# A list scheduler that charges each kind of TensorE tiling change its own delay, in a fused attention and sparse-FFN kernel

## The chip, the cores and the metric

One NeuronCore of a Trainium2 chip runs the whole program. The metric is the device time of one execution in microseconds (us). Before the change it is 773.45 us, the median of three runs (772.93 to 773.46).

## The reference, cut to what matters

```python
xn  = layernorm(x)                                     # x: 2048 x 256, float32
# attention: 8 heads of 32, 2 key/value heads, rotary positions, causal
out = softmax(mask(q @ k.T / sqrt(32))) @ v            # per head
qp, kp = q[..., :3] @ dirs, k[..., :3] @ dirs          # one number a position and head
geo_out = softmax(mask(outer(qp, kp))) @ v             # the "geo" attention
out = (out + head_scales * (geo_out - out)) @ Wo
# feed-forward with ternary weights, 1024 wide
z = xn @ ternary(W_syn).T + b_syn
hidden = where(z >= 102nd largest of its row, relu(z), 0)
ffn = layernorm(xn + hidden @ ternary(W_out).T + b_out)
return x + attention + ffn
```

## The kernel before

**Tiles and stages.** The 2048 positions are 16 tiles of 128, or 4 chunks (`c`) of 512. Per tile, TensorE transposes the normalised input (`xT`), multiplies by the q, k, v weights (`qkv`), and transposes q and k (`qT`, `kT`). To subtract a row maximum in the softmax it first forms all scores once in pieces of up to 512 columns (`S`, line 1110), whose maxima VectorE takes (`red`, lines 929 and 932). The feed-forward has the units `xsT`, `z`, `found`, `hT` and `fo`, and ScalarE and VectorE search each row's threshold between them (`sign`, `pick`, `hide`).

**The attention loop.** A slot is (chunk `c`, key head `g`, `kind`, key tile `j`); there are 160 slots. `kind` 1 is the geo attention, `kind` 0 the ordinary one, and each chunk has both, geo first. In a slot TensorE makes the scores of 4 heads in two `pair`s (two matmuls each: line 1191 for kind 0, line 1195 for geo), ScalarE takes the exponent of each pair (`exp`, line 731), TensorE then does `val` (probabilities times v, line 1209) and `sum` (probabilities times ones, line 1216). `probs` has two buffers, so the exponents of slot n+2 wait for the `sum` of slot n (its semaphore `probs_used`). On the diagonal GpSimd clears a triangle (`cut`, line 608).

**Tilings of TensorE.** The planner knows three modes. "full" is every unit and the ordinary scores. "columns" is `val` and `sum`, whose stationary tile is 32 columns wide, four heads side by side. "rows" is the geo scores, whose contraction is 10 rows; their four heads sit in the row groups 0, 32, 64 and 96.

**What sets the order.** `build_plan()` (line 48) is a list scheduler that runs on the host while the program is built. Its result is the fixed order of the instructions of all five engines, and which PSUM bank each unit uses. Nothing is reordered on the chip: the semaphores only make engines wait. Operations stand in flows (queues of one engine that keep their order); each has a duration, a rank (low goes first) and what it waits for. In each step the head of each flow gets an earliest start, `start = max(ready, clock[eng])`; the earliest over all engines, `first`, chooses the engine; and of the heads of that engine that start within `SLACK` = 120 ns of it the one of lowest rank is placed. Ranks on TensorE: units of attention 0 to 7, `h` units 10, `z` units 11, scores 12, `sum` 12.5, `val` 13. Units have two PSUM banks of their own (`BANKS`); `S` may also use the score banks where the next score waits for something. A hand-over between engines counts `HAND` = 160 ns, one within an engine 40 ns.

A change of mode adds `TURN` to the duration of the operation that was chosen, after the choice is made.

Of the kernel before, what the change touches and what calls it, by code (L numbers as in the profile page):

```python
# [15 lines left out]
HG = H // G  # L16
# [19 lines left out]
BANKS = 2  # L36
PAIRS = 2
HAND = 160
TURN = 110
SLACK = 120  # L40
KINDS = ((1, 0), (1, 0), (1, 0), (1, 0))
ATT_SCALE = float(D) ** -0.5
# [5 lines left out]
def build_plan():  # L48
# [10 lines left out]
    for c in range(NCH):  # L59
        tiles = list(range(TPC * c, TPC * c + TPC))  # L60
        for t in tiles:
            add("stat", "dve", 3, ("stat", t), 650, [("x", c)])
        add("stat", "dve", 3, ("eps", c), 180, [("stat", t) for t in tiles])
        add("prep", "pool", 0, ("rstd", c), 1050, [("eps", c)])
        add("stat", "dve", 3, ("shift", c), 180, [("rstd", c)])
        for t in tiles:
            add("norm", "act", 2, ("xn", t), 400, [("shift", c)])
        for t in tiles:
            old = [("unit", "qT", t - 1, 1), ("unit", "kT", t - 1)] if t else []
            unit("qkv", 2 * c, ("xT", t), 220, [("xn", t)])  # L70
            add("xnT", "act", 1, ("xnT", t), 400, [("unit", "xT", t)] + [("unit", "qkv", t - 1)] * (t > 0), empties=("xT", t))
            unit("qkv", 2 * c, ("qkv", t), 1300, [("xnT", t)] + [("w",)] * (t == 0) + [("unit", "kT", t - 2)] * (t > 1))
            add("rope", "dve", 0, ("rope", t), 1380, [("unit", "qkv", t)] + [("join", t - 1)] * (t > 0),
                empties=("qkv", t))
            add("rope", "dve", 0, ("split", t), 1050, [("join", t), ("q_twin", t)] + old[1:])
            add("twin", "act", 1, ("q_twin", t), 620, [("join", t)] + old[:1])
            add("prep", "pool", 1, ("join", t), 880, [("rope", t)] + [("split", t - 1), ("q_twin", t - 1)] * (t > 0))
            add("prep", "pool", 1, ("geo_dots", t), 1300, [("join", t)] + old[1:])
            for half in range(2):
                unit("heads", 2 * c, ("qT", t, half), 440, [("split", t), ("q_twin", t)])  # L80
            unit("heads", 2 * c, ("kT", t), 440, [("split", t), ("geo_dots", t)])
            wait = [("sum", c - 2, G - 1, 0, TPC * (c - 1) - 1)] if c >= 2 else []
            for half in range(2):
                add("heads", "act", 1, ("q_in", t, half), 590, [("unit", "qT", t, half)] + wait, empties=("qT", t, half))
            add("heads", "act", 1, ("k_in", t), 800, [("unit", "kT", t)] + [("geo_hi", c - 1), ("geo_max", c - 1), ("geo_lo", c - 1)] * (c > 0),
                empties=("kT", t))
        for t in tiles:
            for h in range(H):
                for p in range(c + 1):
                    cols = CHUNK if p < c else (t % TPC + 1) * P  # L90
                    unit("S", 2 * c + 1, ("S", t, h, p), 25 + 0.41 * cols, [("q_in", t, h // HG), ("k_in", t)])
                    add("S", "dve", 1, ("red", t, h, p), 152 + 1.045 * cols + (20 if p == c else 0), [("unit", "S", t, h, p)],
                        empties=("S", t, h, p))
            add("S", "dve", 1, ("mx", t), 180, [("unit", "mT", c - 1)] * (c > 0 and t == tiles[0]))
        unit("S", 0, ("mT", c), 440, [("mx", t) for t in tiles])
        add("S", "dve", 1, ("m", c), 1400, [("unit", "mT", c)] + [("m_dma", c - 1)] * (c > 0), empties=("mT", c))
        add("dma", "sp", 0, ("m_dma", c), 1000, [("m", c)])

        add("geo", "dve", 3, ("scan", c), 2800, [("k_in", t) for t in tiles] + [("geo_top", c - 1)] * (c > 0))
        add("geo", "act", 2, ("geo_hi", c), 1050, [("k_in", t) for t in tiles] + [("geo_dma", c - 1)] * (c > 0))  # L100
        add("geo", "dve", 3, ("geo_lo", c), 1220, [("geo_hi", c)])
        add("geo", "pool", 3, ("geo_max", c), 2650, [("scan", c)])
        add("geo", "dve", 3, ("geo_top", c), 1830, [("geo_max", c)] + [("geo_dma", c - 1)] * (c > 0))
        add("geo", "sp", 1, ("geo_dma", c), 8000, [("geo_top", c), ("geo_lo", c), ("geo_hi", c), ("fill",)]
            + ([("sum", c - 1, G - 1, 1, TPC * c - 1)] if c >= 1 else []))
# [41 lines left out]
    for n, (c, g, kind, j) in enumerate(slots):  # L147
        share = 1 - max(0, j - TPC * c) / TPC
        for pair in range(PAIRS):
            first = [("m_dma", c)] if kind == 0 else [("geo_dma", c)]  # L150
            old = [("exp",) + slots[n - 1] + (pair,)] if n else []
            add("score", "pe", 12, ("score", c, g, kind, j, pair), (475 if kind == 0 else 225) * share + 15, first + old,
                "full" if kind == 0 else "rows")
            add("exp", "act", 0, ("exp", c, g, kind, j, pair), 170 + 855 * share, [("score", c, g, kind, j, pair)]
                + ([("sum",) + slots[n - 2]] if n >= 2 else []))
            if j >= TPC * c:
                add("cut", "pool", 0, ("cut", c, g, kind, j, pair), 440, [("exp", c, g, kind, j, pair)])
        e = epilogues.index((c, g, kind))
        add("val", "pe", 13, ("val", c, g, kind, j), 30 + 870 * share,
            [("cut" if j >= TPC * c else "exp", c, g, kind, j, PAIRS - 1)]  # L160
            + ([("o_raw",) + epilogues[e - 1], ("d_raw",) + epilogues[e - 1]] if j == 0 and e else []), "columns")
        add("val", "pe", 12.5, ("sum", c, g, kind, j), 30 + 870 * share, [("val", c, g, kind, j)], "columns")
    for e, (c, g, kind) in enumerate(epilogues):
        last = [("sum", c, g, kind, TPC * (c + 1) - 1)] + [("mix",) + epilogues[e - 1]] * (e > 0)
        add("epi", "act", 0, ("d_raw", c, g, kind), 600, last)
# [40 lines left out]
    mode = "full"  # L206
# [4 lines left out]
    while left:  # L211
        best = []
        for (eng, flow), keys in queue.items():
            at = heads[(eng, flow)]
            if at == len(keys):
                continue
            key = keys[at]
            rank = ranks[key]
            _, ns, after, m, empties = op[key]
            ready = 0.0  # L220
            ok = True
            if key[0] in ("o_add", "y_out"):
                other = ("y_out" if key[0] == "o_add" else "o_add", key[1])
                if other in done:
                    after = after + (other,)
            if any(d not in done for d in gates.get(key, ())):
                continue
            for d in after:
                if d not in done:
                    ok = False  # L230
                    break
                src = op[d][0] if d in op else "sp"
                ready = max(ready, done[d] + (40 if src == eng else HAND))
            if not ok:
                continue
            if key[0] == "unit":
                spare = [i for i in banks_for(key) if free_from(i) is not None]
                if not spare:
                    continue
                ready = max(ready, min(free_from(i) for i in spare))  # L240
            if key[0] == "score":
                pair = [free_from(BANKS + 2 * key[5] + i) for i in range(2)]
                if None in pair:
                    continue
                ready = max(ready, max(pair))
            start = max(ready, clock[eng])
            best.append((start, rank, key, eng, flow, ns, m))
        first = min(b[0] for b in best)
        close = [b for b in best if b[0] <= first + SLACK and b[3] == min(best)[3]]
        start, rank, key, eng, flow, ns, m = min(close, key=lambda b: (b[1], b[0]))  # L250
        if eng == "pe":
            if m != mode:
                ns += TURN
                mode = m
            if key[0] == "unit":
                i = min((i for i in banks_for(key) if free_from(i) is not None), key=free_from)
                holds[i] = key[1:]
                bank[key[1:]] = i
            if key[0] == "score":
                for i in range(2):  # L260
                    holds[BANKS + 2 * key[5] + i] = key
        clock[eng] = start + ns
        done[key] = clock[eng] + landing.get(key[0], 0)
        plan[eng].append(key)
        heads[(eng, flow)] += 1
        left -= 1
# [990 lines left out]
```

How the kernel before makes its waits and increments, by code:

```python
        def filled(eng, name):  # L453
            eng.wait_ge(side_full, unit_no[name] + 1)
            return bank_of(name)
# [1 line left out]
        def consumed(eng, name):  # L458
            eng.wait_ge(side_free[bank[name]], freed_at[name])
# [12 lines left out]
        @block.sync  # L473
# [20 lines left out]
                    c = key[1]
                    consumed(sp, ("mT", c))
                    for r, rows in enumerate((m_hi, m_lo)):
                        sp.dma_start(q_stack[STK + r:STK + r + 1, c % 2].bitcast(F32),
                                     rows.bitcast(F32)).then_inc(m_in[c], 16)
                if k == "geo_dma":
                    c = key[1]
                    cols = slice(CHUNK * c, CHUNK * c + CHUNK)
                    sp.wait_ge(geo_ready, c + 1)
                    if c == 0:
                        sp.wait_ge(geo_filled, 2)
                    if c >= 1:
                        sp.wait_ge(probs_used, acc_done[epi_no[(c - 1, G - 1, 1)]])
                    for g in range(G):
                        hs_ = slice(HG * g, HG * g + HG)
                        for r, src in enumerate((geo_hi[hs_, 0], geo_lo[hs_, 0], geo_hi[hs_, 0])):
# [11 lines left out]
                if k == "store":  # L524
                    t = key[1]
                    sp.wait_ge(ffn_added, t + 1)
                    consumed(sp, ("o", t))
                    sp.dma_start(out_rows[t], res[:, t]).then_inc(stored, 16)
            sp.wait_ge(stored, 16 * NT)
# [137 lines left out]
            def link(ins):  # L667
                mark(ins)
                act.wait_ge(act_step, steps[0])
```

## Time and profile before

| | us |
|---|---|
| median of the runs (3) | 773.45 |
| the profiled execution | 772.55 |
| its span, first to last instruction | 770.6 |
| TensorE (PE) matmul busy | 699.5 (91%) |
| VectorE (DVE) busy | 499.1 (65%) |
| ScalarE (ACT) busy | 464.7 (60%) |
| GpSimd (POOL) busy | 262.5 (34%) |

The profile is of one execution. PE busy is the union of the matmuls' spans, which overlap each other; so two neighbouring groups of matmuls are best compared by the distance between their starts. L1209 means line 1209 of the kernel. Times in the views count from the start of the span.

### The profile page before, as it was taken

The page shows a single profiled execution, that of the slowest core. Times are in us where ns is not written, and L with a number is a line of the kernel's source. Part 1 is how long each engine was busy: PE and PEld are TensorE (multiplying, and loading weights), DVE is VectorE, ACT ScalarE, POOL GpSimd, SP SyncE. Part 2 cuts the span into 40 slices and gives each one's busy share as a digit, 9 for nine tenths or more (in the row PEclk, how much of TensorE's full clock was granted, in tenths as well). Part 3 has the DMA queues.
Part 4 walks back from the last instruction along what each step waited for, and adds up shares of the span by engine and source line. Part 5 has one row for each costly group of instructions (what it writes and reads, how often), then busy time and mean ns, then how long its engine had stood idle before and what let it go on. Part 6 is the DMA issues. An engine that isn't in the chain of part 4 may idle for free. (4 is left out here: it accounts for less than half of the span.)

```text
span 770.6 us, 12758 instructions
## 1 busy us (share of the span) xinstructions
PE 699.5 (91%) x4536; PEld 327.3 (42%) x4536; DVE 499.1 (65%) x1022; ACT 464.7 (60%) x789; POOL 262.5 (34%) x390
## 2 busy tenths in 40 slices
PE   2766789999999999999999999999899999988993
PEld 1443335333434444443444445444445455553532
DVE  3798478764386886377777873655776666667602
ACT  3352655335753544875443547888889889868650
POOL 5514453332431312331101203324424533356532
PEclk9885889698999999999999999899999999999996
DMA  8100000000000000000000000000000000000000
GB/s 240 61 1 4 6 1 8 1 1 3 1 8 1 1 1 1 3 1 1 6 3 1 1 1 10 1 1 8 16 7 9 8 8 15 8 8 2 1 1 27
DMA packets 12372, 9.40 MB, mean 12 GB/s; under 512 B 5713, under 2 KB 11729, under 8 KB 12306
## 3 DMA queue, kind: packets, MB, share of 16 engines
q1 hardware_dynamic: 12306, 8.55, 3.8%
q8 instruction: 37, 0.61, 0.3%
q14 instruction: 29, 0.24, 0.1%
HBM read 5.80 MB, written 2.10 MB: 10 GB/s over the span
## 5 line engine op out<-in xcount | busy, mean ns | idle before, releaser
L731 ACT ACTIVATE probs<-scores 128x1024 f32<-128x1024 f32 (+3 forms) x320 | 270.0, 893 | 202.9 <-PE acc L1216 188.3
L929 DVE TENSOR_REDUCE piece_max<-side 128x1 f32<-128x512 f32 x192 | 127.9, 686 | 54.5 <-PE side L1110 53.3
L1209 PE MATMUL acc<-probs,v_nat 128*32 128x512 f32 (+3 forms) x1280 | 157.1, 564 | 5.3 <-POOL probs L608 3.9
L1216 PE MATMUL acc<-probs,ones_all 128*32 128x512 f32 (+3 forms) x1280 | 155.4, 558 | 0.0
L608 POOL TENSOR_SCALAR_AFFINE_SELECT probs<-probs 128x256 f32<-128x256 f32 x128 | 56.3, 451 | 184.1 <-ACT probs L731 182.7
L1110 PE MATMUL side<-k_stack,q_stack 96*128 96x512 f32 (+3 forms) x290 | 112.6, 442 | 3.9 <-DVE piece_max L929 3.6
L1191 PE MATMUL scores<-q_stack,k_stack 98*128 98x512 f32 (+3 forms) x320 | 90.2, 384 | 5.6 <-ACT probs L731 5.3
L1110 PEld LDWEIGHTS side<-k_stack,q_stack 96*128 96x128 f32 x290 | 51.4, 194 | 96.2 <-DVE piece_max L929 45.2
L955 DVE RECIPROCAL d_raw<-d_raw 128x512 f32<-128x512 f32 x16 | 53.6, 3347 | 34.7 <-ACT o_raw L744 34.7
L1191 PEld LDWEIGHTS scores<-q_stack,k_stack 98*128 98x128 f32 x320 | 53.0, 190 | 36.0 <-ACT probs L731 27.1
L1195 PE MATMUL scores<-q_geo,k_geo 10*128 10x512 f32 (+3 forms) x320 | 58.0, 468 | 6.6 <-ACT probs L731 6.3
L932 DVE CUSTOM_DVE_ANT_0 side<-side,tail_mask 128x512 f32<-128x512 f32 (+3 forms) x98 | 48.8, 498 | 15.3 <-PE side L1110 14.8
L1209 PEld LDWEIGHTS acc<-probs,v_nat 128*32 128x32 f32 x1280 | 28.8, 110 | 57.0 <-issue 46.2
L1216 PEld LDWEIGHTS acc<-probs,ones_all 128*32 128x32 f32 x1280 | 30.6, 111 | 48.9 <-issue 46.3
L644 POOL TENSOR_TENSOR xb<-xn,b_down 128x256 f32<-128x256 f32 x16 | 12.4, 777 | 108.5 <-DVE y_mv L1062 98.5
L1195 PEld LDWEIGHTS scores<-q_geo,k_geo 10*128 10x128 f32 x320 | 23.3, 183 | 53.6 <-ACT probs L731 34.1
L1087 PE MATMUL side<-w_qkv,xnT 128*128 128x384 f32 x64 | 31.6, 627 | 4.3 <-DVE v_nat L883 1.6
L1044 DVE SCALAR_TENSOR_TENSOR work<-z_buf,thresh 128x1024 f32<-128x1024 f32 x16 | 22.0, 1376 | 17.8 <-DVEq L1041 17.8
L1163 PE MATMUL side<-down_T,h_split 128*128 128x256 f32 x128 | 31.9, 288 | 1.1 <-DVE h_split L1051 1.1
L629 POOL TENSOR_TENSOR o_raw<-o_raw,d_raw 128x512 f32<-128x512 f32 x8 | 10.2, 1276 | 65.9 <-DVE d_raw L955 65.8
L1080 PE MATMUL side<-ident,xn 128*128 128x128 f32 x64 | 14.8, 316 | 19.0 <-ACT xn L678 12.3
L1164 PE MATMUL side<-down_T,h_split 128*128 128x256 f32 x128 | 31.0, 281 | 0.0
(143 smaller groups left out, 1024.5 us busy)
## 6 DMA issues: line engine op xcount, KB each, us to landing
res<-in_L_attn_x_dram SPq DMA_DIRECT2D x4, 512.0 KB, 9.2
out_dram<-res SPq DMA_DIRECT2D x16, 128.0 KB, 1.7
z_buf<-in_L_ffn_W_syn_dram SPq DMA_DIRECT2D x1, 1024.0 KB, 7.7
z_buf<-in_L_ffn_W_out_dram SPq DMA_DIRECT2D x1, 1024.0 KB, 4.8
k_geo<-geo_rows SPq DMA_DIRECT2D x24, 8.0 KB
q_geo<-geo_rows SPq DMA_DIRECT2D x24, 8.0 KB
w_qkv<-in_L_attn_Wq_dram SPq DMA_DIRECT2D x1, 256.0 KB, 4.2
tables<-in_cos_table_dram SPq DMA_DIRECT2D x1, 256.0 KB, 4.5
```

The source lines that it names most:

```text
L608: nc.gpsimd.affine_select(out=tri, in_=tri, compare_op=ALU.is_ge, fill=0.0, base=0, pattern=[[0, 2], [1, P]], channel_multiplier=-1).then_ ...
L731: nc.scalar.activation(probs[:, slot % 2, pair, :, off:], scores[:, pair, :, off:], ACT.Exp, scale=ATT_SCALE if kind == 0 else 1.0).then_i ...
L929: free(nc.vector.tensor_reduce(piece_max[:, h, p:p + 1], pt, AX.X, ALU.max), ("S",) + a)
L932: free(nc.vector.tensor_tensor_reduce(pt[:, 0:ncol], pt[:, 0:ncol], tail_mask[:, CHUNK - ncol:], 1.0, -3.0e38, ALU.add, ALU.max, piece_max ...
L955: nc.vector.reciprocal(d_raw[:], d_raw[:]).then_inc(recip_ready, 1)
L1087: last = nc.tensor.matmul(pt[:, 0:QKV], xnT[:, i], w_qkv[:, i], start=(i == 0), stop=(i == KC - 1))
L1110: last = nc.tensor.matmul(pt[:, 0:ncol], q_stack[0:STK, b, h, col:col + P], k_stack[0:STK, h // HG, CHUNK * p:CHUNK * p + ncol], start=Tru ...
L1163: nc.tensor.matmul(pt[:, 0:C], h_hi[:, i], down_T[:, i], start=(i == 0), stop=False)
L1191: last = nc.tensor.matmul(dst[:, off:], k_stack[:, g, P * j:P * j + P], q_stack[:, b, HG * g + h, off:], start=True, stop=True)
L1195: last = nc.tensor.matmul(dst[:, off:], k_geo[rows, P * j:P * j + P], q_geo[rows, g, off:], start=True, stop=True)
L1209: nc.tensor.matmul(acc[D * h:D * h + D, 0, off:], v_nat[:, j, g], probs[:, slot_no[a] % 2, h // 2, h % 2, off:], start=(j == 0), stop=(j = ...
L1216: last = nc.tensor.matmul(acc[D * h:D * h + D, 1, off:], ones[:, 0:D], probs[:, slot_no[a] % 2, h // 2, h % 2, off:], start=(j == 0), stop ...
```

## The change

The delay becomes a table by the pair of modes (from, to), and it is added to the clock before a start is compared with others, where it used to be added to the duration after the choice. Three kinds of piece get other durations in the plan. No instruction is added or removed and no operand changes; only what the planner thinks, and so the order, the banks of the units, and the semaphore values that follow from it.

```diff
-TURN = 110
+TURN = {("full", "columns"): 235, ("rows", "columns"): 215, ("columns", "full"): 145, ("columns", "rows"): 145,
+        ("full", "rows"): 220, ("rows", "full"): 220}
...
-                    unit("S", 2 * c + 1, ("S", t, h, p), 25 + 0.41 * cols, [("q_in", t, h // HG), ("k_in", t)])
+                    unit("S", 2 * c + 1, ("S", t, h, p), 45 + 0.42 * cols, [("q_in", t, h // HG), ("k_in", t)])
...
-            add("score", "pe", 12, ("score", c, g, kind, j, pair), (475 if kind == 0 else 225) * share + 15, first + old,
+            add("score", "pe", 12, ("score", c, g, kind, j, pair), (480 if kind == 0 else 200) * share + 25, first + old,
...
-        add("val", "pe", 13, ("val", c, g, kind, j), 30 + 870 * share,
+        add("val", "pe", 13, ("val", c, g, kind, j), 15 + 860 * share,
...
-        add("val", "pe", 12.5, ("sum", c, g, kind, j), 30 + 870 * share, [("val", c, g, kind, j)], "columns")
+        add("val", "pe", 12.5, ("sum", c, g, kind, j), 15 + 860 * share, [("val", c, g, kind, j)], "columns")
...
-            start = max(ready, clock[eng])
+            start = max(ready, clock[eng] + (TURN.get((mode, m), 0) if eng == "pe" else 0))
...
         if eng == "pe":
-            if m != mode:
-                ns += TURN
-                mode = m
+            mode = m
```

## Rows read from the trace of the kernel before

**Rows 1.** The page: busy time of each engine, and its share of the span.

```profile
PE 699.5 (91%) x4536; PEld 327.3 (42%) x4536; DVE 499.1 (65%) x1022; ACT 464.7 (60%) x789; POOL 262.5 (34%) x390
```

**Rows 2.** Stages: length; busy of PE, PEld, DVE, ACT, POOL; granted clock; DMA.

```profile
0.00:86.00 86.00, 51.84 (x200) 30.89 (x201) 59.46 (x176) 32.26 (x66) 36.33 (x62) 0.80 0.25 70
...
276.00:474.00 198.00, 196.01 (x1267) 83.66 (x1266) 140.29 (x272) 108.00 (x158) 37.80 (x70) 1.00 0.01 2
474.00:611.00 137.00, 132.73 (x947) 61.99 (x944) 86.51 (x157) 119.38 (x228) 51.28 (x63) 0.96 0.03 8
611.00:680.00 69.00, 67.39 (x451) 35.65 (x449) 46.29 (x90) 60.54 (x114) 27.14 (x31) 0.98 0.03 9
...
751.00:771.00 20.00, 6.54 (x16) 4.98 (x16) 5.05 (x5) 1.06 (x2) 5.36 (x4) 0.65 0.08 26
```

**Rows 3.** Waits of ScalarE: who waited for whom, us in total, times, longest.

```profile
ACT probs L731 <- PE acc L1216: 188.3, 91, 7.4
```

**Rows 4.** TensorE in order of time, ordinary attention of chunk 2: start, us, group.

```profile
400.08 1.06 PE L1216 MATMUL acc<-probs,ones_all 128*32 128x512 f32 x8
401.08 0.61 PE L1110 MATMUL side<-k_stack,q_stack 96*128 96x256 f32 x2
401.62 1.06 PE L1209 MATMUL acc<-probs,v_nat 128*32 128x512 f32 x8
402.62 0.73 PE L1110 MATMUL side<-k_stack,q_stack 96*128 96x512 f32 x2
403.19 1.10 PE L1191 MATMUL scores<-q_stack,k_stack 98*128 98x512 f32 x4
404.13 0.28 PE L1110 MATMUL side<-k_stack,q_stack 96*128 96x256 f32 x1
404.34 1.06 PE L1216 MATMUL acc<-probs,ones_all 128*32 128x512 f32 x8
405.34 0.72 PE L1110 MATMUL side<-k_stack,q_stack 96*128 96x512 f32 x2
405.99 1.07 PE L1209 MATMUL acc<-probs,v_nat 128*32 128x512 f32 x8
```

**Rows 5.** ScalarE in order of time, the two exponents between those.

```profile
396.90 1.94 ACT L731 ACTIVATE probs<-scores 128x1024 f32<-128x1024 f32 x2 [2.82 <-PE acc L1216]
```

**Rows 6.** TensorE in order of time, `sum` and `val` side by side.

```profile
720.34 1.09 PE L1191 MATMUL scores<-q_stack,k_stack 98*128 98x512 f32 x4
721.35 1.06 PE L1209 MATMUL acc<-probs,v_nat 128*32 128x512 f32 x8
722.24 1.04 PE L1216 MATMUL acc<-probs,ones_all 128*32 128x512 f32 x8
723.09 1.04 PE L1209 MATMUL acc<-probs,v_nat 128*32 128x512 f32 x8
```

**Rows 7.** TensorE in order of time, two `S` with full-array work on both sides.

```profile
217.09 0.63 PE L1110 MATMUL side<-k_stack,q_stack 96*128 96x512 f32 x2
217.56 0.63 PE L1191 MATMUL scores<-q_stack,k_stack 98*128 98x512 f32 x2
```

**Rows 8.** TensorE in order of time, first and last of the 92 places.

```profile
93.38 1.71 PE L1216 MATMUL acc<-probs,ones_all 128*32 128x512 f32 x8
...
743.04 1.06 PE L1216 MATMUL acc<-probs,ones_all 128*32 128x512 f32 x8
```

**Rows 9.** TensorE in order of time, geo attention of chunk 3.

```profile
510.72 0.51 PE L1195 MATMUL scores<-q_geo,k_geo 10*128 10x512 f32 x4
511.16 1.07 PE L1216 MATMUL acc<-probs,ones_all 128*32 128x512 f32 x8
...
524.16 0.50 PE L1195 MATMUL scores<-q_geo,k_geo 10*128 10x512 f32 x2
524.60 1.07 PE L1216 MATMUL acc<-probs,ones_all 128*32 128x512 f32 x8
525.59 0.50 PE L1195 MATMUL scores<-q_geo,k_geo 10*128 10x512 f32 x2
```

**Rows 10.** VectorE in order of time beside rows 4; in brackets its idle time before.

```profile
403.15 1.29 DVE L929 TENSOR_REDUCE piece_max<-side 128x1 f32<-128x512 f32 x2 [0.62 <-PE side L1110]
...
405.94 1.29 DVE L929 TENSOR_REDUCE piece_max<-side 128x1 f32<-128x512 f32 x2 [0.71 <-PE side L1110]
```

**Rows 11.** The chain that ended last, its end: start, us, what.

```profile
750.92 10.47 issue
761.38 6.56 PE side L1171 x16
767.97 0.42 DVE res L961
```

## The prediction

> **What bounds the kernel now.** I read the page first. TensorE is busy for 91% of the span, the next engine for 65% [rows 1]. By stages the picture holds where the attention runs: from 276 to 474 us TensorE is busy 196.0 of 198 us, from 474 to 611 us 132.7 of 137, while in the first 86 us, before the attention, it is busy only 51.8 [rows 2]. The waits say the same: ScalarE's largest one, 188.3 us in 91 pieces, is for a `sum` on TensorE that gives a `probs` buffer back [rows 3]. So in the middle of the span whatever shortens TensorE's queue shortens the kernel, and the queue's order is what the change touches. The last 20 us are a fixed tail: 10.47 us without TensorE while the last softmax is normalised, then the output projection [rows 11]. The first 86 us and this tail I leave unchanged: the modes other than "full" hardly occur there.
>
> **What a change of tiling costs.** Read starts, not durations. A `sum` of 512 columns followed by a `val` of 512 takes 0.85 us start to start (722.24 to 723.09) [rows 6]; followed by a full-array unit it takes 1.00 (400.08 to 401.08, 404.34 to 405.34) [rows 4]: leaving columns costs 0.14 to 0.15. Two `S` of 512 between full work take 0.47 (217.09 to 217.56) [rows 7]; the same two between columns take 0.65 (405.34 to 405.99) [rows 4]: 0.18 for both edges. The first `val` after full work takes 0.89, 0.03 to 0.04 more (721.35 to 722.24) [rows 6]. One visit to full work between two column groups thus costs about 0.15 + 0.18 + 0.03 = 0.36 us of TensorE. The old planner counts 2 x 110 = 220 ns for it, the new one 235 + 145 = 380 ns, so the new figure is near the trace.
>
> **What the order will do, part 1: `sum` followed by `val`.** After `sum` of slot n, if the exponents of slot n+1 are done, `val` can start at the clock. Before, a unit that was ready started at the clock too and won by rank. Now it starts at clock + 145, outside the slack of 120, and `val` wins. After `val` the case is different: its `sum` starts at clock + 40, a unit at clock + 145 is within 40 + 120, and still wins by rank. So the new order should read `sum`(n) `val`(n+1), then full work, where the old one made two visits to columns a slot. I walked the whole timeline and counted, over the 160 slots, at how many ends of a `sum` the next `val` had its exponents (and cuts) done more than 160 ns ago and something else was placed: 92 places, the first at 93.38 us and the last at 743.04 [rows 8]. One of them: both exponents end at 396.90 + 1.94 = 398.84 [rows 5], `sum` ends at 401.08, and two `S` go ahead of the `val` at 401.62 [rows 4]. In 79 of the 92 the exponents had been done for over 1 us. If those 79 join: 79 x 0.356 = 28.1 us (0.356 is the 0.36 above with one digit more, from the same starts over all such groups). All 92 would give 32.7, none gives 0.
>
> **Part 2: what pays for it.** The units that leave those gaps must go elsewhere, and in 50 of the 92 places they are two `S`. They use two banks, which come free only when VectorE has reduced them, 1.29 us for two [rows 10]. Inside one longer stretch of full work the third and fourth unit wait for banks, and the new planner accepts this: it leaves full work only if nothing there starts within 235 + 120 = 355 ns, where the old one waited up to 120. I take the middle of 120 and 355, 0.24 us, once for each of the 50 moved pairs: +12.0 us. Bounds: 0, if scores cover the wait (four score matmuls take 0.94 us, 403.19 to 404.13) [rows 4], up to 50 x 0.355 = 17.8. VectorE itself is not the limit: it idles 0.62 and 0.71 us before a pair of reductions for want of `S` [rows 10], and is busy 140 of 198 us in that stage [rows 2].
>
> **Part 3: geo pairs.** The two pairs of a geo slot sit in different row groups and run at once: both take 0.44 us together (510.72 to 511.16), but one alone takes 0.43 to 0.44 as well (524.16 to 524.60) [rows 9]. A split pair costs one more 0.43. The 160 pairs are placed in 106 visits to rows where 80 would do, so 26 are dear: 11.2 us. When `val`(n+1) goes first, both exponents of slot n+1 are over, so both pairs of slot n+2 can start together; and from rows the planner now waits up to 215 + 120 = 335 ns for the second one. I take 40% of it, -4.5 us, between 0 and -11.2.
>
> **Part 4: ScalarE.** From 474 to 611 us it is busy 119.4 of 137 us, and to 680 us 60.5 of 69: 87 and 88% [rows 2]. 27 of the 79 places lie after 474 us, worth 9.6 us. ScalarE has room for that on average, but its queue is in order and `sign` work stands between exponents, so I give back half: +4.8 us, between 0 and 9.6. A rule speaks for giving back: the Trainium skill, TensorEngine Tiling, "PSUM Bottleneck", says that tiling speeds TensorE up but not the emptying of PSUM, which may then become the limit. Taken strictly after 474 us it would make this term 9.6 and the sum 4.8 less; the trace so far shows TensorE late there, not ScalarE.
>
> **Part 5: the new piece times.** `S` of 512 goes from 235 to 260 ns, `val` and `sum` from 900 to 875, geo scores from 240 to 225, ordinary from 490 to 505. These move the planner's clock by up to 25 ns a piece and change only near ties. Nothing on the chip takes longer for it; I take 0 and allow 4 us to either side for the luck of another order.
>
> **The sum.** -28.1 + 12.0 - 4.5 + 4.8 = -15.8 us. The profiled execution took 772.55 us (span 770.6 and 1.95 around it), so 756.8; the median of the runs is 0.9 above it, so I predict 757.7 us. Span: about 755.
>
> **Rivals.** *A, the waits win (slower).* The planner now idles rather than turns. The old order has 187 changes from full to columns and 60 from rows to columns. If many of them are preceded by a wait for a unit, the price is up to 0.235 us more each than the old rule allowed; the place is the stage of `S` units, where banks come back one at a time, and later the feed-forward chain `hT`, `fo`. It decides from 28.1 / 187 = 0.15 us a change on: at 0.18 us, 33.7 - 28.1 = 5.6 us slower, 779 us. For it: the waits sit on the engine that is the bound. Against it: a wait is only planned where a unit is near, and saves 0.36 later. Chance 0.14. *B, ScalarE takes over.* All gain after 474 us is lost and geo pairs stay as they are: 52 x 0.356 = 18.5 minus 12.0, 6.5 us, 767 us. For it, 87% busy; against it, its 188.3 us of waits for TensorE [rows 3]. Chance 0.20. *C, the joins undo themselves.* The scores of slot n+2 now come after `val`(n+1), so its exponents are later, and the next `sum` finds them unfinished and leaves columns again: only each second place joins, 14 us, against the same 12.0: 771 to 772 us, no change that can be told. Against it: over 1 us of room in 79 places, and `val` takes 0.86. Chance 0.11. *D, all of it comes.* 32.7 + 11.2 with waits hidden behind scores and 4 us of them left: 40 less, 734 us; with half the geo gain 740. Chance 0.15. My forecast, 750 to 764 us, has 0.40.
>
> **How the numbers follow.** About 0.2% (1.5 us) is what a measurement of this kernel can tell from no change. Faster: 0.40 + 0.20 + 0.15 + half of C, 0.05 = 0.80. Same: half of C, 0.06. Slower: 0.14. The range takes in B and C above and, with part of A left out, ends at 776; below it takes in half of D, 741.
>
> **What would show it.** In the changed kernel's timeline, L1216 followed directly by L1209 much more often than the 30 times it was, and two `S` between `sum` and `val` mostly gone; visits to columns down from 247 towards 170; geo scores mostly as x4; visits to rows down from 106 towards 90. TensorE's idle time waiting for L929 and L932 may rise by about 10 us. ScalarE's waits for L1216 should fall in total. The prediction is wrong if the number of changes hardly falls, if TensorE's waits grow by as much as the changes give back, or if the feed-forward chain (last `fo` now 18 us before the last `val`) ends after the attention.

## The result: 1.9% slower, where 2.0% faster was forecast

The changed kernel takes 786.78 us (median of 5 runs, 786.27 to 787.87). The kernel before, beside it, took 772.93; the ratio is 1.0187, with a 95% interval of 1.0172 to 1.0202. The profiled execution has a span of 784.3 us against 770.6, so there are 13.7 us to explain. Runs of these kernels scatter by some us from one execution to the next (the kernel before between 768 and 778 us in all rounds), so below each kernel is compared by its ratio to the kernel before in the same rounds.

Line numbers are one lower from line 250 on: L1109 is the `S` of L1110, L1208 and L1215 are `val` and `sum`, L1194 and L1190 the scores.

**The changes of tiling fell as forecast.** Walking the timeline, `sum` is followed at once by `val` 106 times against 30. Visits to columns went from 247 to 176, all changes of mode from 609 to 495. TensorE in order of time, at the start of the stage from 276 to 474 us, now reads:

```profile
277.16 0.73 PE L1109 MATMUL side<-k_stack,q_stack 96*128 96x512 f32 x2
277.73 0.51 PE L1190 MATMUL scores<-q_stack,k_stack 98*128 98x384 f32 x2
278.18 1.06 PE L1215 MATMUL acc<-probs,ones_all 128*32 128x512 f32 x8
279.06 1.04 PE L1208 MATMUL acc<-probs,v_nat 128*32 128x512 f32 x8
```

The `sum` at 278.18 and the `val` at 279.06 stand side by side, 0.88 us apart; in [rows 4] it was 1.00, two `S`, and then the `val`.

**And yet TensorE is not done earlier.** First the changed kernel's page, then three stages of it (length; busy of PE, PEld, DVE, ACT, POOL; granted clock; DMA):

```profile
PE 708.6 (90%) x4536; PEld 337.9 (43%) x4536; DVE 498.0 (63%) x1022; ACT 467.0 (60%) x789; POOL 264.2 (34%) x390
```

```profile
86.00:276.00 190.00, 180.23 (x1134) 80.83 (x1136) 135.90 (x285) 94.28 (x147) 64.49 (x112) 0.90 0.01 3
276.00:474.00 198.00, 192.40 (x1216) 84.02 (x1209) 130.42 (x251) 104.53 (x148) 39.48 (x69) 0.97 0.01 2
474.00:745.00 271.00, 258.65 (x1813) 130.18 (x1813) 166.96 (x307) 223.83 (x413) 114.70 (x137) 0.96 0.02 7
```

and the same stages of the kernel before; its row from 276 to 474 us, clock 1.00, is in [rows 2]:

```profile
86.00:276.00 190.00, 181.24 (x1179) 78.31 (x1179) 124.99 (x261) 98.64 (x154) 68.27 (x118) 0.91 0.01 3
...
474.00:745.00 271.00, 258.08 (x1812) 126.90 (x1812) 169.28 (x310) 222.20 (x408) 112.29 (x131) 0.97 0.02 7
```

In the same 198 us TensorE got 1216 matmuls done in place of 1267, was busy 3.6 us less, and ran at 0.97 of its clock in place of 1.00; in the 190 us before, 1134 in place of 1179. Matmuls differ in size, so I also weighed each group by its own time (defined below): by 276 us the changed kernel has 2.4 us less of TensorE's work behind it than the kernel before, by 474 us 10.3 less, by 745 us 12.2 less. Most of the loss falls in the stage of `S` units. One stretch shows the slow work at its plainest:

```profile
336.00:350.00 14.00, 13.03 (x98) 5.95 (x98) 12.48 (x26) 6.47 (x11) 6.20 (x9) 1.00 0.00 1
350.00:357.00 7.00, 7.00 (x22) 2.47 (x26) 5.62 (x9) 1.80 (x3) 0.00 (x0) 0.52 0.00 0
```

From 350 to 357 us the clock is at its lower level of 1.2 GHz, and TensorE, busy all the time, does 22 matmuls. The timeline around it (idle time before a group in brackets):

```profile
343.28 0.61 PE L1208 MATMUL acc<-probs,v_nat 128*32 128x256 f32 x8
344.16 0.76 PE L1109 MATMUL side<-k_stack,q_stack 96*128 96x512 f32 x2 [0.26 <-DVE piece_max L928]
344.84 0.51 PE L1194 MATMUL scores<-q_geo,k_geo 10*128 10x512 f32 x4
345.44 0.93 PE L1109 MATMUL side<-k_stack,q_stack 96*128 96x512 f32 x2
...
354.56 1.94 PE L1208 MATMUL acc<-probs,v_nat 128*32 128x512 f32 x8
```

Here is the wait that grew: TensorE stands before an `S` until VectorE has reduced what was in its bank. At 344.16 it has just left columns for it. The two `S` at 345.44 take 0.86 us to the next group's start, for 0.65 between columns in [rows 4], and less than 0.15 us of it is idle on record. The `val` at 354.56 takes 1.94 us for 1.06.

The profile's own list of TensorE's waits shows little of this, since neighbouring matmuls overlap and a short wait hides in the busy time. From 86 to 745 us its idle time before an `S`, before and after the change, is:

```profile
PE side L1110 <- DVE piece_max L929: 3.6, 8, 1.0
PE side L1109 <- DVE piece_max L928: 6.6, 13, 2.0
```

With the 0.7 us for L931 that makes 3.7 us more, and all waits of TensorE in this window together are the same (23.5 and 23.6 us). So the waits have to be looked for in the distances between starts.

**The balance.** I took for each of the 1182 groups the distance to the next group's start, and as its own part the 10th percentile for its type and size; the usual surplus for the modes around it (the 25th percentile at full clock) is the cost of changes, what is left is waiting, and all surplus where the clock was low is counted apart. In us, over the whole span:

| | own | changes | waits at full clock | surplus at half clock |
|---|---|---|---|---|
| before | 513.8 | 117.7 | 63.4 | 58.2 |
| changed | 513.8 | 97.9 | 84.8 | 70.6 |
| difference | 0 | -19.8 | +21.4 | +12.4 |

The sum, +14.0, must come near the span's +13.7, because the own parts are the same; it is no test of the split. Of the waits, those that end in an `S` went from 10.9 to 22.0; by stage, waits grew by 6.1 us (86 to 276 us), 12.8 (276 to 474) and 4.1 (474 to 745). Of 316 units that take a bank after an `S`, 92 started within 260 ns of the end of the reduction that frees it, and now 147 do ("tight" below). This split is mine, worked out from one execution of each; the times of the experiments below don't depend on it. Drawn with other percentiles, other neighbours and another limit for "low clock", the same two traces give 13 to 30 us less for changes, 15 to 34 more for waits and 8 to 12 more at half clock. The signs hold, the sizes don't.

### The profile page after: what moved, and what is told of

Its sections match the earlier page's. It is cut to its first block, busy times and chain, and to the rows that moved or that the text cites. A ratio compares the mean times of both kernels' runs of the same rounds, so it can differ in the third digit from the quotient of the medians.

```text
span 784.3 us, 12758 instructions
## 1 busy us (share of the span) xinstructions
PE 708.6 (90%) x4536; PEld 337.9 (43%) x4536; DVE 498.0 (63%) x1022; ACT 467.0 (60%) x789; POOL 264.2 (34%) x390
## 4 chain that ended last, share of the span: by engine, by line
PE 47%; DVE 6%; issue 4%; ACT 3%; POOL 3%; DVEq 0%; ACTq 0%; POOLq 0%
PE acc L1208 10%; PE acc L1215 10%; PE scores L1190 6%; PE side L1109 5%; PE scores L1194 3%; PE side L1162 2%; PE side L1145 2%; DVE piece_max L928 2%; PE side L1163 2%; PE side L1153 2%; PE side L1170 2%; ACT probs L730 2%; PE side L1146 2%; PE side L1147 1%; PE side L1086 1%
## 5 line engine op out<-in xcount | busy, mean ns | idle before, releaser
L730 ACT ACTIVATE probs<-scores 128x1024 f32<-128x1024 f32 (+3 forms) x320 | 270.6, 893 | 203.3 <-PE acc L1215 185.4
L1208 PE MATMUL acc<-probs,v_nat 128*32 128x512 f32 (+3 forms) x1280 | 159.0, 571 | 5.0 <-POOL probs L607 3.7
L1215 PE MATMUL acc<-probs,ones_all 128*32 128x512 f32 (+3 forms) x1280 | 156.4, 562 | 0.0
L1109 PE MATMUL side<-k_stack,q_stack 96*128 96x512 f32 (+3 forms) x290 | 116.7, 454 | 10.1 <-DVE piece_max L928 6.6
L1190 PE MATMUL scores<-q_stack,k_stack 98*128 98x512 f32 (+3 forms) x320 | 91.4, 388 | 3.3 <-ACT probs L730 3.2
L1109 PEld LDWEIGHTS side<-k_stack,q_stack 96*128 96x128 f32 x290 | 52.7, 197 | 87.7 <-DVE piece_max L928 39.1
L1208 PEld LDWEIGHTS acc<-probs,v_nat 128*32 128x32 f32 x1280 | 36.9, 114 | 82.3 <-issue 65.7
L1190 PEld LDWEIGHTS scores<-q_stack,k_stack 98*128 98x128 f32 x320 | 52.7, 189 | 37.0 <-ACT probs L730 30.5
L1194 PE MATMUL scores<-q_geo,k_geo 10*128 10x512 f32 (+3 forms) x320 | 56.5, 484 | 3.9 <-ACT probs L730 3.4
L931 DVE CUSTOM_DVE_ANT_0 side<-side,tail_mask 128x512 f32<-128x512 f32 (+3 forms) x98 | 48.8, 498 | 13.9 <-PE side L1109 13.5
L1215 PEld LDWEIGHTS acc<-probs,ones_all 128*32 128x32 f32 x1280 | 30.4, 113 | 50.9 <-issue 48.7
L1194 PEld LDWEIGHTS scores<-q_geo,k_geo 10*128 10x128 f32 x320 | 23.0, 190 | 41.0 <-ACT probs L730 23.2
L1162 PE MATMUL side<-down_T,h_split 128*128 128x256 f32 x128 | 33.2, 296 | 0.5 <-DVE h_split L1050 0.4
L1043 DVE SCALAR_TENSOR_TENSOR work<-z_buf,thresh 128x1024 f32<-128x1024 f32 x16 | 21.9, 1366 | 17.8 <-DVEq L1040 17.8
L1163 PE MATMUL side<-down_T,h_split 128*128 128x256 f32 x128 | 31.8, 285 | 0.0
```

Source lines behind the costliest of these rows:

```text
L730: nc.scalar.activation(probs[:, slot % 2, pair, :, off:], scores[:, pair, :, off:], ACT.Exp, scale=ATT_SCALE if kind == 0 else 1.0).then_i ...
L931: free(nc.vector.tensor_tensor_reduce(pt[:, 0:ncol], pt[:, 0:ncol], tail_mask[:, CHUNK - ncol:], 1.0, -3.0e38, ALU.add, ALU.max, piece_max ...
L1109: last = nc.tensor.matmul(pt[:, 0:ncol], q_stack[0:STK, b, h, col:col + P], k_stack[0:STK, h // HG, CHUNK * p:CHUNK * p + ncol], start=Tru ...
L1162: nc.tensor.matmul(pt[:, 0:C], h_hi[:, i], down_T[:, i], start=(i == 0), stop=False)
L1163: last = nc.tensor.matmul(pt[:, 0:C], h_lo[:, i], down_T[:, i], start=False, stop=(i == NN - 1))
L1190: last = nc.tensor.matmul(dst[:, off:], k_stack[:, g, P * j:P * j + P], q_stack[:, b, HG * g + h, off:], start=True, stop=True)
```

## The experiments

All are held against the kernel before in the same rounds; ratios have their 95% interval. "Changes" are changes of mode in the plan.

**1. The two halves of the rule.** The delay counts in the comparison only when TensorE leaves columns (`join_only`), or only when it leaves the others (`wait_only`):

```diff
+            turn = TURN.get((mode, m), 0) if eng == "pe" else 0
-            start = max(ready, clock[eng] + (TURN.get((mode, m), 0) if eng == "pe" else 0))
+            start = max(ready, clock[eng] + (turn if mode == "columns" else 0))   # wait_only: mode != "columns"
...
         if eng == "pe":
+            if not (mode == "columns"):                                          # wait_only: !=
+                ns += TURN.get((mode, m), 0)
             mode = m
```

> The delay counts in the comparison of starts only when TensorE leaves columns (so val follows sum), and is charged after the choice when it leaves full or rows (so no longer waits are accepted there). The plan has 510 changes of tiling and 191 visits to columns, against 609 and 247 before, 495 and 176 after. Theory (the accepted waits cost the time, the joins save it): the 99 changes saved at 0.17 us give 17 us and no wait is added, 752 to 764 us. Rival (putting val before the next scores is itself what costs): 780 us or more.

> The reverse: the delay counts in the comparison only when TensorE leaves full or rows, and is charged after the choice when it leaves columns. 558 changes, 217 visits to columns. Theory (the accepted waits cost): 51 changes saved give 9 us, waits as in the changed kernel cost 20 us and the half clock about 10: 785 to 795 us. Rival (the joins cost): 765 to 775 us.

`join_only`: 784.45 us, 1.0151 (1.0091 to 1.0211). `wait_only`: 796.6 us, 1.0284 (1.0226 to 1.0342). The waiting half alone is the worst of all kernels, as my theory asks, and just above its forecast of 785 to 795; 158 of its units are tight. But the joining half missed its forecast of 752 to 764 and falls by number into the rival. Its end on TensorE shows where the time went (here `val` and `sum` are L1211 and L1218, and the other lines are shifted alike):

```profile
742.37 0.40 PE L1218 MATMUL acc<-probs,ones_all 128*32 128x128 f32 x8
...
756.22 6.26 PE L1173 MATMUL side<-w_o,mixed 128*128 128x256 f32 x16 [5.79 <-issue]
762.41 0.19 PE L1125 MATMUL side<-ones_all,found 128*1 128x1 f32 x2
765.82 1.94 PE L1156 MATMUL side<-ident,work 128*128 128x128 f32 x8 [3.22 <-DVE work L1046]
769.25 0.55 PE L1165 MATMUL side<-down_T,h_split 128*128 128x256 f32 x1 [1.49 <-DVE h_split L1053]
```

The attention's last `sum` (L1218) comes at 742.4 us, 8 us earlier than before the change; the output projection (L1173) at 756, 5 us before that of [rows 11]. But `hT` (L1156) and `fo` (L1165) of the feed-forward's last two tiles are still to come, and TensorE waits between them. From the last `sum` to the end it takes 38 us, where the kernel before takes 20. The last `S` was at 485.5 us, for 461.2 before; the `z` units of the feed-forward stand behind it in rank, on VectorE its threshold search too, and I read the late chain from that; no run tests it, and `start90` below has its last `S` as late (484.1) without this tail (its last `fo` ends at 757).

That the joins speed TensorE up is not shown. About 5 us of its work, two times `hT` and `fo`, has only moved from before the last `sum` to behind it. Weighed by own time, `join_only` has 4.4 us less work behind it than the kernel before at 474 us and 6.1 less at 611, long before the tail. My forecast of 17 us for the joins alone is refuted, and the rival is not excluded.

**2. The size of the delay without the new place, and the piece times alone.**

```diff
-            start = max(ready, clock[eng] + (TURN.get((mode, m), 0) if eng == "pe" else 0))
+            start = max(ready, clock[eng])
...
         if eng == "pe":
+            ns += TURN.get((mode, m), 0)
             mode = m
```

This edit of the changed kernel is `table_duration`.

> The table of delays and the new piece times, but the delay is charged after the choice, as the single one was. 596 changes of tiling. Theory (the place where the delay is added matters, not its size): 769 to 777 us, as before. Rival (the larger delays shift the plan's clock against the other engines, and that costs): 782 us or more.

> The kernel before with the new piece times alone; 592 changes of tiling. Theory: a few us of luck to either side, 768 to 777 us. Rival (the new piece times bring the loss): 782 us or more.

`table_duration`: 787.32 us, 1.0174 (1.0119 to 1.0229), against my theory: the larger numbers cost the same 1.7% where no wait is accepted and the changes hardly fall (596). So "the place is the cause" fell. `newpieces_only` (the four duration edits alone): 775.26 us, 1.0038 (1.0004 to 1.0073), a small part at most.

What the loss of `table_duration` consists of is less clear. Its stage from 276 to 474 us reads:

```profile
276.00:474.00 198.00, 195.49 (x1197) 82.43 (x1195) 131.07 (x257) 103.63 (x152) 39.98 (x69) 0.94 0.01 2
```

Its granted clock there is 0.94, lower than in the changed kernel, and from 86 us to the last `sum` it runs 75 us at the lower level, as long as the changed one. In a split like the one above, most of its loss is surplus at half clock and hardly any a wait for `S` banks at full clock.

**3. Hold the banks for a shorter time, with the order untouched.**

```diff
-  free(nc.vector.tensor_reduce(piece_max[:, h, p:p + 1], pt, AX.X, ALU.max), ("S",) + a)
+  free(nc.vector.tensor_reduce(piece_max[:, h, p:p + 1], pt[:, 0:P], AX.X, ALU.max), ("S",) + a)
```

> The kernel before, order untouched, but each maximum over a full piece reads only the first 128 of its 512 columns, so its softmax maxima are not the reference's; VectorE holds the bank of such an S for about 0.3 us in place of 0.69. It is the base for the same edit in the changed kernel. Theory (waits for S banks make the loss): 2 to 6 us faster than before, 766 to 771 us. Rival: the same.

> The changed kernel, order untouched, with the same shortened maxima. Theory (the new order packs S units until their banks stop it, TensorE waits there and loses its clock): the loss against before_short shrinks from 14 us to 4 or less, 768 to 774 us, and the half-clock stretches between 276 and 474 us go. Rival (the loss comes from the order elsewhere, and the banks are not its cause): still 10 us or more behind before_short, 778 us or more.

> The kernel with the table charged after the choice (787 us), order untouched, with maxima over 128 of 512 columns as in before_short, so its maxima are not the reference's. Theory (its loss is in waits for banks too): within 6 us of before_short, 766 to 777 us. Rival (another cause): 781 us or more.

`before_short`: 771.07 us, 0.9947 (0.9918 to 0.9976). `after_short`: 772.25 us, 0.996 (0.9927 to 0.9993). The loss of 1.9% against the original is 0.1% by these ratios with short reductions (each has an interval of 0.3% to either side; the means of the ten runs, 769.1 and 771.7 us, are 0.3% apart), though each still runs its own order. The edit also takes 75 us of work off VectorE (busy 499.1 and then 424.3 us), so it does not tell a bank held for a shorter time from a VectorE that is less busy. `tabdur_short`: 777.26 us, 1.004 (1.0013 to 1.0068), so 0.9% behind `before_short` where it had been 1.7%: about half of that kernel's loss does not go with the long reductions. My detail on the clock did not hold: `after_short` still has some 10 us at the lower clock between 276 and 474 us, and its profiled execution is 9.8 us longer than that of `before_short`, whose runs fall into two groups around 765 and 771 us. The medians carry the verdict, not the traces.

**4. The size of the delay, at the new place.** One delay of 110 (`uniform_start`), three quarters of the table (`table75`), the table with the old piece times (`oldpieces`):

```diff
-TURN = {("full", "columns"): 235, ("rows", "columns"): 215, ("columns", "full"): 145, ("columns", "rows"): 145,
-        ("full", "rows"): 220, ("rows", "full"): 220}
+TURN = {(a, b): 110 for a in ("full", "columns", "rows") for b in ("full", "columns", "rows") if a != b}
+# table75: 176, 161, 109, 109, 165, 165
```

> The changed kernel with one delay of 110 ns for all changes, still added before starts are compared, with the new piece times: 595 changes of tiling, 237 visits to columns. Theory (the size of the delays costs, through the waits that it accepts): 768 to 776 us. Rival (the place costs at any size): 782 us or more.

> The changed kernel with the table at three quarters (176, 161, 109, 165 ns), delay before the comparison: 562 changes, 228 visits to columns. Theory (loss grows with the size of the delays): between 768 (all 110) and 787, 772 to 782 us. Rival (the result jumps about with the order): outside that.

> The changed kernel with the old piece times: 501 changes, 182 visits to columns. Theory: the table is the cause, so 780 us or more, as the changed kernel. Rival (order luck of a few ns a piece decides): below 777 us.

`uniform_start`: 767.81 us, 0.9896 (0.9864 to 0.9929). `table75`: 780.63 us, 1.0086 (1.0056 to 1.0117). `oldpieces`: 781.23 us, 1.0077 (1.0055 to 1.01). With the full table at 1.0187 the time rises with the size: round trips of 220, 285 and 380 ns in the plan give -1.0%, +0.9% and +1.9%. But these are three orders and not one mechanism in three sizes. The 109 ns of `table75` for leaving columns lie within the slack of 120, so the joins don't come: its plan has `sum` directly before `val` 38 times, `uniform_start` 35 times, the changed kernel 106. `table75` thus loses without the joins; and without more time at the lower clock, which is 51 us from 86 us to the last `sum`, as in the kernel before.

Four kernels with the new piece times make a square:

| | 110 for all | the table |
|---|---|---|
| charged after the choice | 1.0038 (`newpieces_only`) | 1.0174 (`table_duration`) |
| counted before starts are compared | 0.9896 (`uniform_start`) | 1.0187 (changed kernel) |

The table costs 1.4 points in the old place and 2.9 in the new one. The new place gives 1.4 points with the small delay and nothing with the table. `oldpieces` shows that 1% of the loss goes with the piece times once the table is there, more than they cost alone.

**5. Tell the planner that a bank comes free later.**

```diff
-            return max(done[r] for r in emptied_by[holds[i]]) + HAND
+            return max(done[r] for r in emptied_by[holds[i]]) + HAND + (100 if i < BANKS else 0)
```

> The changed kernel with one more number in the plan: the two banks of the units count as free 100 ns later than the reader's end and the hand-over. 501 changes of tiling, 179 visits to columns. Theory (units placed right behind the reduction that frees their bank cost the time): fewer than 147 units start within 260 ns of that end, and with the changes still saved it is 760 to 772 us. Rival (few changes of tiling lose by themselves): 780 us or more.

> The kernel before, with the banks of the units counted free 100 ns later in the plan; 615 changes of tiling, 242 visits to columns. Theory (the margin mends what the large delays in the comparison broke): no gain here, 770 to 778 us. Rival (the margin is good for any order): 768 us or less.

> The table charged after the choice (787 us), with the same margin; 619 changes of tiling. Theory (waits for banks, there too, since the slower clock of the plan's TensorE brings the units closer to the end of the reductions): 772 to 780 us. Rival (a part of its loss is not in the banks, as its short maxima left 0.9%): 782 us or more.

`margin100` (the changed kernel with this line): 770.12 us, 0.9941 (0.9902 to 0.9981). On the kernel before: 767.75 us, 0.9951 (0.9923 to 0.9978). On `table_duration`: 774.2 us, 1.0009 (0.9989 to 1.0029). The line is worth 2.4 points on the changed kernel, 1.7 on the one with the large delays after the choice, and 0.5 on the one before: it helps most where the loss is. On the kernel before I had forecast nothing, and there the rival came true: the margin helps a little everywhere. Its changes stay at 501, so few changes of tiling don't lose by themselves. Fewer units are tight (133 for 147; 112 for 129; 74 for 92).

**6. Somewhat smaller delays.** `start90` has the table at 0.9, `SLACK` 90 and `HAND` 180; `t90m60` the table at 0.9 and a margin of 60.

```diff
+TURN = {("full", "columns"): 212, ("rows", "columns"): 194, ("columns", "full"): 130, ("columns", "rows"): 130,
+        ("full", "rows"): 198, ("rows", "full"): 198}
...
+            return max(done[r] for r in emptied_by[holds[i]]) + HAND + (60 if i < BANKS else 0)
```

> The changed kernel with the table at 0.9 of its size, a slack of 90 and a hand-over of 180 ns: 493 changes, 184 visits to columns, so the joins of the changed kernel, and a wait of at most 302 ns in place of 355. Theory (joins gain, accepted waits lose): fewer waits, 762 to 772 us. Rival (any order with so few changes loses): 780 us or more.

> The changed kernel with the table at 0.9 of its size and a margin of 60 ns; 489 changes, 178 visits to columns. Theory (joins kept, waits cut): 758 to 769 us, the fastest so far. Rival (the results scatter with the order by more than this): 772 us or more.

`start90`: 768.31 us, 0.9927 (0.99 to 0.9954). `t90m60`: 764.12 us (762.54 to 764.5), 0.9879 (0.9853 to 0.9904), the fastest of all, some 23 us below the changed kernel with the same rule and nearly the same number of changes (489).

By the same balance `t90m60` has 95.8 us of changes, 75.3 of waits and 60.1 at half clock: the saving of the changed kernel, with 20 us of its new cost gone. Its order was picked among some dozens by replaying plans on the host, so a part of its gain may be a lucky order.

Two limits hold for all six. The number of tight units does not order the kernels: `t90m60` has 136 and `uniform_start` 115, both faster than the kernel before with its 92; the changed kernel has 147 and `table75` 144. So the count is a sign of the mechanism and no measure of it. And every kernel is a single order. How far the time scatters over orders that are equally good in the plan is not measured, so a step of half a per cent between two of them says little about its cause.

## Why the prediction was wrong, step by step

**The bound** (TensorE in the middle of the span) holds: it is still busy 192.4 of 198 us from 276 to 474 us and 258.7 of 271 after it, VectorE 130.4 and 167.0. But the time on it depends on when VectorE gives the banks back, as the short reductions show.

**A change of tiling** at 0.36 us a round trip agrees with the split, no more: 114 fewer changes saved 19.8 us, 0.17 a change, 0.35 for two, and other ways to draw the split give 0.11 to 0.26 a change.

**Part 1, the joins:** they came, 76 more of them for the 79 forecast. Their worth of 28.1 us was too high: 71 visits fewer, not 79, and the measured 19.8 us include all kinds of change.

**Part 2 is the step that failed, the price of the waits.** "I take the middle of 120 and 355, 0.24 us, once for each of the 50 moved pairs: +12.0 us." The waits grew by 21.4 us, above my upper bound of 17.8, and I had counted only the pairs that a join moves. The term is short by 9.4 us. Between the forecast (-15.8) and the split (+14.0) lie 29.8 us, and three more terms make up the rest: joins and geo pairs were to save 32.6 us and saved 19.8 (12.8), the clock was not in the sum (12.4), and the 4.8 us that I gave back for ScalarE did not come.

What the experiments show in its place: the larger delays act on every choice. `table_duration`, which accepts no longer wait and joins hardly anything, loses 1.7%, `table75`, without the joins, 0.9%. A margin on the banks wins it back in both kernels that it was tried on, and short reductions win back nearly all of the changed kernel's loss. How it comes about is my reading, not shown: the plan's TensorE runs slower against the plan's VectorE, banks look free sooner in terms of TensorE's work, and units, which have the lowest ranks, are placed right behind the reductions everywhere. The remaining half in `tabdur_short` says it isn't only the `S` banks, and what holds the rest stays open.

**What the sum lacked altogether** is the clock: +12.4 us of surplus at half clock, about as much as the loss itself. I had no term for it; in the kernel before, the stage from 276 to 474 us ran at 1.00, and I took that as given. That new waits bring the low clock is seen only side by side here: no kernel of mine changed the clock and left the waits, so it isn't shown as cause and effect. Three numbers on record speak for care. `table75` loses 0.9% with no more time at the lower level than before. `margin100` has a lower granted clock than the kernel before (median 0.928 of ten runs, 0.931 beside it) and is 0.6% faster. And the kernel before, always the same order, took 771.9 us in the median of its 27 runs at a clock of 0.940 and 776.3 in that of its 8 runs at 0.925: 23 us more at the lower level go with 4.4 us. By that ratio the changed kernel's 24 us more would be worth about 5 us, an estimate, where my split has 12.4.

**Part 3:** visits to rows fell from 106 to 101, not towards 90; worth about 2 us, not 4.5. **Part 4:** ScalarE did not take over: 223.8 us busy of 271 against 222.2, and it still waits 185.4 us for L1215, after 188.3. Rival B is out. The rule that I took from the Trainium skill, TensorEngine Tiling, "PSUM Bottleneck", that the emptying of PSUM may become the limit, does not describe ScalarE here. For VectorE it fits in part: TensorE waits more for `S` banks to be emptied, but VectorE is busy for only 130 of 198 us there, so the time of each hand-over counts and not VectorE's throughput. **Part 5:** within its 4 us alone (0.38%, 3 us), but up to 1% together with the table.

**The rivals:** A came true, with its place (the stage of `S` units) and its kind (slower), not with its price. The waits alone, 21.4 us over its 187 changes, are 0.11 us a change and under its threshold of 0.15; only with the 12.4 us at half clock is it 0.18. A also measured itself against the 28.1 us of Part 1, of which less came. I gave it 0.14, on the argument that a planned wait is only placed where it pays. That trusts the plan's clock to some tens of ns. C is out (the joins stayed), D too. Of the signs that I named, TensorE's idle time for L929 and L932 rose by 3.7 us in the profile's list, not by 10. The feed-forward's end, which I named as a thing that would make the prediction wrong, did so in `join_only`, not in the changed kernel.

## What to carry to other kernels

A list scheduler with truer costs need not give a better order: its optimism may have been slack that the waits on the chip needed. When costs are made exact, give the hand-overs of scarce buffers a margin (here 100 ns on two banks turned 1.9% slower into 0.6% faster, and 60 ns with the table at 0.9 into 1.2%), and try the rule and its numbers apart. Price a reordering by the waits that it adds on the bound engine over all choices, not only at the places where it does what it is meant to, and ask what those waits do to TensorE's clock.

## What the hardware showed that I had not expected

TensorE's granted clock fell to its lower level of 1.2 GHz from 350.3 to 357.1 us of the changed kernel, although from the `val` at 343.28 on it had stood idle for only 0.57 us in all and never over 0.26 us at a stretch. What it did in that time was short `S` pieces between waits, short pieces of `val` and `sum`, and geo scores, which are only 10 rows high. Which of these matters no run shows. Between 86 us and the last `sum` about 51 us of the kernel before and 75 us of the changed one ran at that level.
